# State space layer: nine of 48 sum units on ScalarE and GpSimd, two of them in a chunk's first half, and the convolution's first term on ScalarE

## The reference

```python
xz = xs @ in_proj_w.T                       # 384 -> 2 x 768
xin, z = split(xz)
xc = depthwise causal convolution of xin over L, 4 taps
xin = silu(xc + conv_b)
dt, Bm, Cm = split(xin @ x_proj_w.T)        # 24, 16, 16
dt = softplus(dt @ dt_proj_w.T + dt_proj_b)
A = -exp(A_log)                             # 768 x 16
def step(h, (x_t, dt_t, B_t, C_t)):
    h = exp(dt_t * A) * h + dt_t * B_t * x_t    # 768 x 16
    return h, sum over the 16 states of h * C_t
y = (ys + xin * D) * silu(z)
out = layernorm(y @ out_proj_w.T) * gamma + beta
```

## Time and profile before

| what | us |
|---|---|
| median of three runs | 5354.77 (5343.97 to 5362.83) |
| the profiled execution | 5347.93 |
| its span, first to last instruction | 5346.1 |
| TensorE, VectorE, ScalarE, GpSimd busy | 4686.3, 4381.3, 3070.4, 2970.7 |
| mean granted TensorE clock | 0.962 of 2.4 GHz |

### The profile page before, as it was taken

How to read it: one execution, slowest core, us unless ns; L and a number is a source line. 1 busy time by engine, 2 the same in 40 slices (tenths; PEclk the granted TensorE clock), 3 DMA queues, 4 the chain that set the end, 5 groups by cost and what they waited for, 6 DMA issues and landing times.

```text
span 5346.1 us, 78656 instructions
## 1 busy us (share of the span) xinstructions
PE 4686.3 (88%) x28623; PEld 3835.5 (72%) x28623; DVE 4381.3 (82%) x4965; ACT 3070.4 (57%) x6391; POOL 2970.7 (56%) x3552
## 2 busy tenths in 40 slices
PE   4888888888888888888888886779998899999999
PEld 2666666666666666666666665446877799999999
DVE  1999999999999999999999999677677765665555
ACT  3777777777777777777777774333332223333333
POOL 3776777777777777777777775456554520000000
PEclk8999999999999999999999999889797988999999
DMA  2001000001000001000000001110201021112110
GB/s 78 1 13 33 10 10 10 10 11 35 10 10 10 10 11 35 10 10 10 10 10 10 10 5 44 44 32 20 92 20 41 26 72 53 54 51 60 45 60 29
DMA packets 96933, 148.64 MB, mean 28 GB/s; under 512 B 5748, under 2 KB 93604, under 8 KB 96548
## 3 DMA queue, kind: packets, MB, share of 16 engines
q1 hardware_dynamic: 96548, 143.63, 8.4%
HBM read 101.00 MB, written 42.61 MB: 27 GB/s over the span
## 4 chain that ended last, share of the span: by engine, by line
PE 50%; issue 15%; DVE 15%; POOL 12%; ACT 7%; DMA 1%; POOLq 0%; DVEq 0%; SPq 0%; ACTq 0%
PE pw L1776 8%; PE pw L1763 6%; PE pw L462 6%; PE pw L451 6%; DVE a_h L744 5%; POOL a_dBT L882 4%; PE ps L413 3%; PE ps L353 3%; DVE b_cv L1393 3%; PE ps L373 2%; DVE a_acc L763 2%; PE ps L1763 2%; POOL a_xin L834 2%; POOL a_acc L894 2%; PE pw L1176 2%
## 5 line engine op out<-in xcount | busy, mean ns | idle before, releaser
L744 DVE TENSOR_TENSOR_SCAN a_h<-a_dA,pw 128x771 f32<-128x771 f32 x1152 | 2015.7, 1752 | 125.6 <-PE pw L451 124.6
L600 ACT ACTIVATE a_dA<-a_dt,a_Aneg 128x384 f32<-128x384 f32 x2304 | 1345.5, 607 | 155.0 <-DVE a_h L744 150.1
L462 PEld LDWEIGHTS pw<-g_ident,a_h 128*128 128x128 f32 x6912 | 786.6, 142 | 619.8 <-DVE a_acc L763 267.1
L882 POOL TENSOR_SCALAR a_dBT<-a_dtxT,a_BC 128x768 f32<-128x768 f32 x1152 | 1026.2, 909 | 300.7 <-PE pw L451 216.6
L462 PE MATMUL pw<-g_ident,a_h 128*128 128x128 f32 x6912 | 983.1, 279 | 227.5 <-DVE a_acc L763 158.1
L451 PE MATMUL pw<-g_ident,a_dBT 128*128 128x128 f32 x6912 | 958.9, 276 | 4.8 <-POOL a_dBT L882 4.8
L763 DVE SCALAR_TENSOR_TENSOR a_acc<-pw,a_BC,a_acc 128x768 f32<-128x768 f32 x912 | 915.3, 1004 | 52.5 <-PE pw L462 48.1
L451 PEld LDWEIGHTS pw<-g_ident,a_dBT 128*128 128x128 f32 x6912 | 806.5, 143 | 6.5 <-POOL a_dBT L882 5.5
L834 POOL TENSOR_TENSOR a_xin<-a_xin,a_tm 128x384 f32<-128x384 f32 x432 | 433.3, 1003 | 34.2 <-ACT a_tm L521 9.0
L1887 DVE TENSOR_TENSOR d_hf<-d_hf,d_wb 128x384 f32<-128x384 f32 x288 | 159.1, 557 | 312.4 <-ACT d_hf L1819 300.2
L894 POOL TENSOR_TENSOR a_acc<-a_acc,a_tm 128x768 f32<-128x768 f32 x168 | 307.4, 1830 | 171.1 <-ACT a_tm L614 170.2
(11 more groups left out here) (228 smaller groups left out, 9377.7 us busy)
## 6 DMA issues: line engine op xcount, KB each, us to landing
d_wb<-cw SPq DMA_DIRECT2D x24, 768.0 KB, 5.7
a_xs<-in_x SPq DMA_DIRECT2D x24, 576.0 KB, 3.9
x<-a_xs SPq DMA_DIRECT2D x24, 576.0 KB, 3.0
b_x<-x SPq DMA_DIRECT2D x24, 576.0 KB, 4.4
b_xs<-x SPq DMA_DIRECT2D x24, 576.0 KB, 5.0
e_xs<-x SPq DMA_DIRECT2D x24, 576.0 KB, 3.8
out<-e_xs SPq DMA_DIRECT2D x24, 576.0 KB, 5.8
a_sx<-in_x SPq DMA_DIRECT2D x54, 192.0 KB, 2.3
```

The costliest lines, as they stand in the source:

```text
L462: t = e.transpose(m["pw2"][:, c * 128:(c + 1) * 128], m[f"a_h{g % 2}"][:, c // 2, first_col(c) + tb * 128:first_col(c) + (tb + 1) * 128], ...
L600: e.activation(dA[:, first_col(c):first_col(c) + T], m[f"a_dt{k % 2}"][:, c, :], ACT.Exp, scale=m["a_Aneg"][:, c, n:n + 1]).then_inc(s["a_ ...
L744: e.tensor_tensor_scan(m[f"a_h{g % 2}"][:, p % 3, :], m[f"a_dA{pi % NDA}"][:], m[f"pw{pi % 2}"][:, COL:COL + PAIR], 1.0, ALU.mult, ALU.add ...
L882: t = e.tensor_scalar(m[f"a_dBT{g % 2}"][:, tb, :], m[f"a_dtxT{o}"][:, tb, :], m[f"a_BC{o}"][:, tb, n:n + 1], 1.0, ALU.mult, ALU.mult)
```

## The change

Two further units, 6 and 13, go to ScalarE and GpSimd in all chunks but those in which statistics are taken (2, 8 and 14), with a product tile of their own, `a_tm13`, which lies over `a_sx` and the start of `a_dt3`. The first tap of the convolution (with its bias) moves from GpSimd to ScalarE, which now issues four instructions for each channel group; the semaphore counts and the due times change with it. The first statistics load of an image now also waits for GpSimd's last sum unit of the chunk before.

```diff
--- before.py
+++ after.py
@@ -47,7 +47,7 @@
 d_xs0 d_xs1 d_xs2 d_sx d_x1o0 d_x1o1 d_x1o2
 p_const p_dt p_xn p_cv p_halo p_dtx p_sz p_pow p_dbt p_st p_gn
 pe_b pe_h pe_A pe_P pe_O pe_Z pe_X pe_BC pe_V pe_G pe_T pe_gn
-a_A a_exp a_raw a_pr a_xi a_sz a_gz a_x a_bc a_v a_sp a_dtx a_beta a_ob a_ln a_cw p_cw
+a_A a_exp a_raw a_pr a_c0 a_xi a_sz a_gz a_x a_bc a_v a_sp a_dtx a_beta a_ob a_ln a_cw p_cw
 v_w v_scan v_acc v_dt3 v_D v_ln v_g v_st
 d_x00 d_x01 d_x02 d_x03 d_x04 d_x05 d_x10 d_x11 d_x12 d_x13 d_x14 d_x15 d_t0 d_t1 d_t2 d_l1 d_l2 d_x3o
 p_zero p_na p_sw p_nb p_c2 p_g p_gn1 p_gn2 p_gn3
@@ -162,10 +162,13 @@
     m.new("a_Wdt3", [128, DI], F32R)
     m.new("a_raw", [128, 6, T + 3])
     m.new("a_xn", [128, 3, T])
-    m.new("a_sx", [128, T])
     m.new("a_dt0", [128, 6, T])
     m.new("a_dtxT0", [128, TB, DI])
     m.new("a_xs0", [128, 3, T])
+    at = m.at
+    m.new("a_tm13", [128, DI])
+    m.section(at)
+    m.new("a_sx", [128, T])
     m.new("a_dt3", [128, T], F32R)
     m.new("a_tm0", [128, T])
     at = m.at
@@ -314,13 +317,27 @@
 T_AT = (78.6, 79.8, 81, 85.6, 86.6, 87.6)
 Z_AT = (63.5, 67.5, 71.5, 75, 82, 88.8)
 
-LENT = (20, 22, 24, 26, 38, 41, 43)
+LENT, EARLY = (20, 22, 24, 26, 38, 41, 43), (6, 13)
+
+
+def has_stats(k):
+
+    return k % NQ == 2 and k // NQ + 1 < NB
+
+
+def lent_units(k):
+
+    return () if k == NCH else LENT if has_stats(k) else EARLY + LENT
+
+
+def is_lent(hh):
+    return hh >= 0 and hh % PAIRS in lent_units(hh // PAIRS)
 
 
 def lent(hh):
 
-    k, u = divmod(hh, STEPS // 2)
-    return len(LENT) * k + sum(x < u for x in LENT)
+    k, u = divmod(hh, PAIRS)
+    return sum(len(lent_units(i)) for i in range(k)) + sum(x < u for x in lent_units(k))
 
 
 def chunk(k):
@@ -454,7 +471,7 @@
     def turned(hh):
         g, tb = divmod(hh, TB)
         w.wait_ge("v_scan", 3 * g + 3)
-        if hh > 0 and (hh - 1) % PAIRS in LENT:
+        if is_lent(hh - 1):
             w.wait_ge("a_cw", lent(hh))
         else:
             w.wait_ge("v_acc", hh - lent(hh))
@@ -511,16 +528,21 @@
         w.wait_ge("p_halo", k + 1)
         w.wait_ge("a_raw", 6 * k + i + 1)
         w.wait_ge("pe_BC", k)
-        for j in range(1, 4):
-            yield 6.2 + 5.4 * i + j
+        for j in (1, 2, 0, 3) if i == 0 else (0, 1, 2, 3):
+            yield 6.2 + 5.4 * i + 0.8 * j + (2 if i == 0 and j in (0, 3) else 0)
+            if j == 0:
+                w.wait_ge("p_sz", 6 * (k - 2) + i + 1)
+                w.wait_ge("p_dtx", 6 * (k - 1) + i + 1)
+                e.activation(m[f"a_xin{o}"][:, i, :], raw[:, i, 0:T], ACT.Identity, scale=pv[:, i, 0:1], bias=pv[:, i, 4:5]).then_inc(s["a_c0"], 1)
+                continue
             pr = 18 * k + 3 * i + j - 1
             if pr >= NTM:
                 kb, rb = divmod(pr - NTM, 18)
-                w.wait_ge("p_cv", 24 * kb + 4 * (rb // 3) + rb % 3 + 2)
+                w.wait_ge("p_cv", 18 * kb + rb + 1)
             w.wait_ge("p_cw", lent(PAIRS * (k - 1)))
             e.activation(m[f"a_tm{pr % NTM}"][:], raw[:, i, j:j + T], ACT.Copy, scale=pv[:, i, j:j + 1]).then_inc(s["a_pr"], 1)
     yield 39.5
-    w.wait_ge("p_cv", 24 * (k + 1))
+    w.wait_ge("p_cv", 18 * (k + 1))
     e.activation(m[f"a_xin{o}"][:], m[f"a_xin{o}"][:], ACT.Silu).then_inc(s["a_xi"], 1)
     if k > 0:
         silu_gate(e, m, w, k - 1)
@@ -529,6 +551,8 @@
     w.wait_ge("pe_X", k + 1)
     w.wait_ge("pe_V", 6 * k)
     w.wait_ge("pe_BC", k)
+    if k > 0:
+        w.wait_ge("p_cw", lent(PAIRS * (k - 1) + EARLY[-1] + 1))
     e.activation(m["a_dt3"][:], pd[:, 0:T], ACT.Copy).then_inc(s["a_x"], 1)
     e.activation(m["a_tm0"][32:64, :], pd[32:64, 0:T], ACT.Copy).then_inc(s["a_x"], 1)
     yield 57.3
@@ -609,9 +633,13 @@
         hh = PAIRS * k + u
         w.wait_ge("pe_h", hh + 1)
         w.wait_ge("a_bc", k + 1)
-        w.wait_ge("p_cv", 24 * min(k + 2, NCH))
+        if u in EARLY:
+            w.wait_ge("v_st", GN * min(k // NQ + (k % NQ > 2), NB - 1) + 18)
+            w.wait_ge("pe_V", 6 * (k + 1))
+        else:
+            w.wait_ge("p_cv", 18 * min(k + 2, NCH))
         w.wait_ge("p_cw", lent(hh))
-        e.activation(m["a_tm12"][:], m["pw2"][:, 0:DI], ACT.Copy, scale=m[f"a_BC{k % 2}"][:, tb, 16 + r:17 + r]).then_inc(s["a_cw"], 1)
+        e.activation(m["a_tm13" if u in EARLY else "a_tm12"][:], m["pw2"][:, 0:DI], ACT.Copy, scale=m[f"a_BC{k % 2}"][:, tb, 16 + r:17 + r]).then_inc(s["a_cw"], 1)
 
     march([pre_act(e, m, w, 0), gate_act(e, m, w, 0)], 0)
     for idx in range(LEAD):
@@ -621,7 +649,7 @@
         side += [pre_act(e, m, w, k + 1), gate_act(e, m, w, k + 1)] if k + 1 < NCH else [last_gate_act(e, m, w)]
 
         def main(n):
-            if n % 2 == 0 and n // 2 - TB - 1 in LENT:
+            if n % 2 == 0 and n // 2 - TB - 1 in lent_units(k):
                 weighed(k, n // 2 - TB - 1)
             exp(STEPS * k + n + LEAD)
 
@@ -746,7 +774,7 @@
     def weighed(hh):
         g, tb = divmod(hh, TB)
         k, r = divmod(g, NS)
-        if hh % PAIRS in LENT:
+        if is_lent(hh):
             return
         acc, ps, cs = m[f"a_acc{k % 2}"][:, tb, :], m["pw2"][:, 0:DI], m[f"a_BC{k % 2}"][:, tb, 16 + r:17 + r]
         w.wait_ge("pe_h", hh + 1)
@@ -756,7 +784,7 @@
             w.wait_ge("v_w", 7)
             e.tensor_scalar(acc, ps, cs, None, ALU.mult).then_inc(s["v_acc"], 1)
         else:
-            if (hh - TB) % PAIRS in LENT:
+            if is_lent(hh - TB):
                 w.wait_ge("p_cw", lent(hh - 2))
             else:
                 w.wait_ge("v_acc", hh - 2 - lent(hh - 2))
@@ -807,6 +835,7 @@
 
     raw = m["a_raw"]
     w.wait_ge("a_pr", 18 * k)
+    w.wait_ge("a_c0", 6 * k)
     if k % NQ == 0:
         e.memset(raw[:, :, 0:3], 0.0).then_inc(m.s["p_halo"], 1)
     else:
@@ -818,19 +847,13 @@
     s, o, pv, raw = m.s, k % 2, m["a_pv"], m["a_raw"]
     xin, dt = m[f"a_xin{o}"], m[f"a_dt{o}"]
     for i in range(6):
-        yield 7.5 + 5.4 * i
-        n = 24 * k + 4 * i
-        w.wait_ge("a_raw", 6 * k + i + 1)
-        w.wait_ge("p_halo", k + 1)
-        w.wait_ge("v_st", 18)
-        w.wait_ge("p_sz", 6 * (k - 2) + i + 1)
-        w.wait_ge("d_w0", 96)
-        e.tensor_scalar(xin[:, i, :], raw[:, i, 0:T], pv[:, i, 0:1], pv[:, i, 4:5], ALU.mult, ALU.add).then_inc(s["p_cv"], 1)
         for j in range(1, 4):
-            yield 7.5 + 5.4 * i + j
+            yield 7.5 + 5.4 * i + j + (1.5 if i == 0 else 0)
             pr = 18 * k + 3 * i + j - 1
+            w.wait_ge("a_c0", 6 * k + i + 1)
             w.wait_ge("a_pr", pr + 1)
-            w.wait_ge("p_cv", n + j)
+            if j > 1:
+                w.wait_ge("p_cv", pr)
             e.tensor_tensor(xin[:, i, :], xin[:, i, :], m[f"a_tm{pr % NTM}"][:], ALU.add).then_inc(s["p_cv"], 1)
     yield 38.5
     if k + 1 < NCH:
@@ -891,7 +914,7 @@
         hh, acc = PAIRS * k + u, m[f"a_acc{k % 2}"][:, u % TB, :]
         w.wait_ge("a_cw", lent(hh) + 1)
         w.wait_ge("v_acc", hh - 2 - lent(hh - 2))
-        e.tensor_tensor(acc, acc, m["a_tm12"][:], ALU.add).then_inc(s["p_cw"], 1)
+        e.tensor_tensor(acc, acc, m["a_tm13" if u in EARLY else "a_tm12"][:], ALU.add).then_inc(s["p_cw"], 1)
 
     march([scale_pool(e, m, w, 0)], 0)
     march([xn_pool(e, m, w, 0)], 0)
@@ -910,7 +933,7 @@
             side.append(xn_pool(e, m, w, k + 2))
 
         def main(n):
-            if n % 2 and (n - 3) // 2 - TB in LENT:
+            if n % 2 and (n - 3) // 2 - TB in lent_units(k):
                 added(k, (n - 3) // 2 - TB)
             if n < STEPS and n % 6 == 0:
                 scaled(NS * k + n // 6 + 1)
@@ -948,6 +971,7 @@
     def stats(b, i):
         q, c = divmod(i, 3)
         w.wait_ge("v_st", GN * (b - 1) + 18 if i == 0 else GN * b + i)
+        w.wait_ge("p_cw", lent(PAIRS * (NQ * (b - 1) + 2)))
         e.dma_start(m["a_sx"][:], xv[b, :, c, q * T:(q + 1) * T]).then_inc(s["d_sx"], 16)
 
     load(0)
```

## The result

The changed kernel takes 5374.14 us (median of 20 runs, 5354.97 to 5379.51), the kernel before 5358.24 beside it (20 runs, 5341.73 to 5367.25): ratio 1.0028, interval 1.0018 to 1.0038, some 15 us slower. The forecast said 42 us slower. The profiled execution took 5374.24 us, its span is 5372.5.

The account below looks back on a forecast made before the run. TensorE, by a hair, bounds the stretch holding units 6 and 13; a late SiLU delays the chunk. 39.7 - 3.4 - 3.6 + 4.1 + 5 = +41.8 on 5347.93 gave 5389.7 us (5397 with the median's offset), range 5349 to 5432.

Parts of the forecast that it names:

- unit 6 is worth nothing: Unit 6 leaving VectorE inside the stretch where TensorE sets the pace: worth 0.
- the place and kind of unit 13's cost: GpSimd's add waits for ScalarE's product, delaying convolution adds and SiLU: 2.09 us a chunk, +39.7 us over 19.
- first term: First tap moved to ScalarE: 0 within a chunk, -3.4 us in the first chunk's convolution ahead of the loop.
- the step on TensorE's clock: At the jam's wait for the third output copy: more TensorE idle time loses the clock more surely, +4.1 and +5 us.
- +4.1: Chunks 4, 10 and 16 would likely lose TensorE's clock too, at 1.37 us each.
- +5: Scans slipping further at the jam through a longer low clock: 0.3 us for 16 chunks, bounds 0 and 29.
- two clock terms: The +4.1 us for three more chunks losing TensorE's clock and the +5 us for longer low clock in 16.
- the ends: Chunk 0 and the last chunk, where two units each leave VectorE at 0.91 us: -3.6 us.
- the waits added: New waits of the loads' queue, the early unit's tile and ScalarE's exponentials: all 0.

Follow-up runs that it names:

- e2: Changed kernel with unit 6 as the only early unit; ratio 0.9988 to the kernel before.
- e1: Changed kernel without its early units, so only the first tap goes to ScalarE; ratio 0.9986 to the kernel before.
- e7: e1 with 16 spare transposes on TensorE ahead of the x projection, which nothing reads; ratio 0.9944 to the kernel before.
- e5: Kernel before with 16 spare transposes on TensorE ahead of the x projection of each chunk from 1 on; ratio 0.9956.
- e6: Changed kernel with 24 spare transposes on TensorE ahead of the x projection; ratio 1.0018 to the kernel before.
- e4: Changed kernel with unit 15 in place of unit 13 as early unit; ratio 0.9996 to the kernel before.
- e13: Kernel before with 16 spare transposes on TensorE ahead of the output projection in each of 23 chunks; ratio 1.0033.
- e16: Changed kernel with 8 spare transposes on TensorE ahead of the output projection in chunk 5 alone; 5381.36 us, one run.
- e14: Changed kernel with 8 spare transposes on TensorE ahead of the output projection in each chunk; ratio 1.0088 to the kernel before.
- e10: Kernel before run again unchanged, for a second profiled execution; 5346.76 us.
- e15: Kernel before with 16 spare transposes on TensorE ahead of the output projection in chunk 5 alone; 5338.65 us, one run.
- e11: Changed kernel run again unchanged, for a second profiled execution; 5366.91 us.
- e3: Changed kernel with unit 13 as the only early unit; ratio 1.0037 to the kernel before.
- e12: e1 with the third output copy issued two steps sooner in ScalarE's order; 5302.98 us, ratio 0.9912 to the kernel before.

## Why the prediction was right and wrong

**Right: unit 6 is worth nothing.** e2 and e1 are 0.0002 apart. That TensorE sets the pace there is the reading of the window, and no run contradicts it in ordinary chunks.

**Right: the place and kind of unit 13's cost.** GpSimd's wait ahead of the add (2.38 us, forecast 2.33), ScalarE's idle time ahead of the SiLU, ended by the last convolution add (1.06, forecast 1.3), the longer wait at the copy (3.05, forecast over 3). The size was 1.80 us a chunk for 2.09. From the add of unit 13 to the end of the last convolution add it is 7.57 us, forecast 7.61; but the forecast then added the 0.25 us that had stood between that add and the SiLU, as if it were a delay of the hand-over. It was ScalarE's own lateness before, and the SiLU now follows within 0.03. Over 19 chunks: 34 us for the 39.7 forecast.

**Right: first term.** 0 within the chunk (SiLU 45.40 for 45.50 in e1), and -2.7 us ahead of the first chunk in the profiled pair, -3.2 in e7 against e5, for -3.4.

**Wrong: the step on TensorE's clock.** This is the failed step: "+4.1" and "+5", both with the sign of a longer wait that loses the clock more surely. In the profiled pair the sign is the other: 12 chunks fewer lose it, at 1.7 us each (133.0 against 131.3), about -20 us. The chunks that keep it went from 131.28 to 133.10, which is 34.6 us for 19. 34.6 - 20.4 = +14.2, and the 19 chunks measured +13.8. Without that, the result would have been near the 33 us of e6 against e5. The forecast without its two clock terms is 39.7 - 3.4 - 3.6 = 32.7. That this is so close is partly luck: unit 13's price was 5.5 us too high over the 19 chunks, the ends were priced 3 us too low (below), and 3 to 4 us of the 33 are e6's longer filling. The price of a lost clock was off as well: 1.37 us from the scan's waits, where the chunks differ by 1.7. The three chunks that I had named as losing the clock, 4, 10 and 16, kept it. The reasoning compared one kept and one lost chunk, found the scan's waits different, and didn't look at TensorE's own wait in the kept one. Its timeline in chunk 4 of the kernel before has

```profile
724.30 0.91 PE L381 MATMUL ps<-a_xin,a_WxT 128*128 128x384 f32 x2 [2.01 <-ACT a_ob L490]
```

2.01 us with the clock kept, where chunk 5 has 2.00 with it lost. The wait's length alone could not be the cause; that row was there to be read. When the wait falls matters (e4, and e13 to e16). The Trainium skill, "TensorE: Matmul & The Clock Gate", section "What's actually happening", says that the windows in which the chip watches TensorE's activity run freely and don't start with the kernel. The prediction took from that section only that idle time lowers the clock; the falls 133.12 us apart, e13 and e14 agree with the part it left out. That chunks of some 133 us come back to the same place each time, so that whatever happens there repeats (lost in the kernel before, kept in the changed one), is argued from the chunk lengths and the spacing of the falls, not tested further.

**Wrong, small: the ends.** -1.8 us each were forecast, both on the ground that VectorE, or at least not TensorE, bounds them. Chunk 0 became 0.9 us longer. The clock isn't in that: no low clock stands in chunk 0 in the kernel before, e10 and e15, which have 123.8 us for it, nor in the changed kernel, e11, e14 and e16, which have 124.7 or 124.8. The prediction didn't look at the SiLU there. In the changed kernel it stands 2.01 us idle for the last convolution add in chunk 0 too, and starts 41.97 us after the first sum for 40.68. Unit 6 did help there: without it (e3, no low clock either) chunk 0 takes 125.3. The last chunk has +0.2 in the profiled pair, but the clock falls in it 118.9 us after its first sum before, and 114.1 after. Where it falls at 114 to 115 in both, it takes 121.1 and 121.0 (e10, e15) against 119.9 and 119.7 (after, e11): -1.3. So the ends gave -0.4 us in place of -3.6.

**Right: the waits added.** The chunks with statistics take 141.4 to 144.3 us in the four profiles of the two kernels, with the SiLU at 47.62 in both; the waits added cost nothing there that these profiles show.

## What to carry to other kernels

- An operation moved to an engine with spare time still takes a place in that engine's order. Look at what is queued behind it: here a 1.83 us add that waits 2.38 us stood ahead of three adds on the critical path. Relief counts only where the relieved engine has no idle time behind the instruction.
- Before a difference under one per cent is given to an edit, compare TensorE's granted clock stretch by stretch. A loop whose every turn has a wait of TensorE can lose or keep the clock in most of its turns; here 0.8 us more in its length turned 4 of 19 into 14 (e14). Remove the wait (e12) or fill it (e5, e7), and then judge the edit.
- The better lever was the order of one copy: e12, without either early unit, is 1.2% ahead of the changed kernel (0.9912 for 1.0028).

## What the runs showed of the hardware

- Waits of TensorE of 2.00 and 2.01 us, with the same work around them, one followed by a clock of 0.61 over 4.4 us and one by 1.00; waits of 3.05 us that kept it in 15 of 19 chunks and, with 0.8 us more per chunk elsewhere, lost it in 14 of 19; waits of 3.02 us that lost it in 16 (e4).
- Falls of the clock 133.12 us apart in chunks that last 133.00 and 132.93 us, so that they move against the work.
- A chunk that loses the clock there is 1.7 us longer; with added work that puts the wait elsewhere, more than half of the added time came back (e13: +16 us for 38 of work).
- The outcome repeats for the most part between executions of one kernel: chunks 1, 3, 9 and 15 in both profiles of the changed one, whose chunk 0 began 0.8 us apart, and 14 of the 16 in the second profile of the kernel before, where it began 2.0 us apart.
